# A two-layer gated cross-attention and expert kernel: five program blocks become one, groups of four tiles become groups of two and four

## The chip, the cores and the metric

The kernel runs on one core of one Trainium2 chip. The core has a matrix engine (PE in the profile; its weight loads are PEld), a vector engine (DVE), a scalar engine (ACT), GpSimd (POOL), a queue processor for transfers (SP), and 16 DMA engines. The metric is the device time of one execution in microseconds, taken as the median of several runs.

## The reference, cut to what matters

64 sequences of 64 positions with 128 features (`x`), a context of the same shape, and a mask of 64 x 64 x 64. Four steps, each added to `x`:

```python
x = x + tanh(g_xattn[0]) * L0_xattn(layernorm(x), ctx, ctx, mask)   # 16 heads of 8, masked softmax
x = x + tanh(g_ffn[0])   * L0_ffn(layernorm(x))                     # 8 experts 128->512->128, top 1, exact gelu
x = x + tanh(g_xattn[1]) * L1_xattn(layernorm(x), ctx, ctx)         # 16 heads of 8, no mask
x = x + tanh(g_ffn[1])   * L1_ffn(layernorm(x))                     # 16 experts 128->64->128, top 2, 8 slots each
```

In `L0_ffn` a token goes to the expert with the largest gate logit. In `L1_ffn` each sequence gives every expert 8 slots; a token that comes too late gets the expert's last slot back in the collecting step.

## The kernel before

The 4096 tokens are 32 tiles of 128 rows; a tile holds two sequences. The program is a row of blocks, and at the end of a block all engines meet: `setup` (constants), `attention(0)`, `experts0`, `attention(1)`, `moe1`. Within a block each engine has a fixed, in-order list of instructions; semaphores tie the engines together.

**Attention.** The list of an engine is made by `run`: step `(f, every, skew)` does its part for tile t at iteration t + skew. Tiles are loaded and projected in groups of Q = 4. SP loads `x`, `ctx` and the mask. DVE makes the layer norm's sums (`stat`), POOL the factors (`norm`), ACT applies them (`normed`), PE turns the tile (`turn_x` L524), ACT copies it out of the matrix engine's memory, PE multiplies by wq (L565). The context is loaded with tokens on the partitions, turned on PE (`turn_ctx` L532), copied by ACT, and multiplied by wk (L570) and wv (L580). POOL spreads the keys into a block form (`k_blk` L290). `score` (L593, L599): in layer 0 two products of 128 x 128 with the identity write the mask's bias over all of `S_ps`, then four products of 64 x 64 add the scores, one for each half of the queries and of the heads. In the profile a product of f32 is two MATMUL records and a product of bf16 one, so the four are eight records. DVE takes the maximum (L409) and subtracts it (L417), PE turns the result (L610), ACT takes the exponential (L372), PE multiplies by the values (L621), DVE divides (L424, L428), PE turns and projects (L629, L635), DVE adds to `x_all` (L437). The scores have one buffer: the next `score` waits for the subtraction of this tile.

**Router.** 8 to 20 iterations behind, each group is normed again, turned (L543), multiplied by the router (L549); DVE picks the expert (`choose`), PE counts (L555, L557), DVE makes the destination rows, and POOL scatters the normed rows to an expert-sorted array in HBM (`scatter` L310, an indirect transfer).

**experts0.** DVE makes tables of the 39 row tiles (L705 to L732), SP and ACT write zero rows behind each expert's last one (L762, L808), then a rolled loop over the 39 tiles: SP loads rows, PE turns them, POOL copies the expert's first weight (`f_w_now` L784), PE multiplies (L823), DVE adds the bias, ACT takes gelu, PE multiplies (L832), DVE adds, SP stores to `expert_out`. The expert weights (4 MB and more) are loaded by SP in four transfers early in `attention(0)` (L251).

**attention(1)** first fetches: 32 indirect transfers on POOL (L258) gather each token's row of `expert_out` and add it into `x_all`. **moe1**: at its start DVE finds all tokens' slots and ACT all exponentials (L1010), then for 32 tiles `move` builds a 0/1 matrix (POOL `one`, DVE `dispatch`) and multiplies the tile by it (PE L1053); 16 steps of experts (L1067, L1078) follow each half, and `back` brings the results to the tokens.

## Time and profile before

| what | value |
|---|---|
| median of 3 runs | 669.02 us (665.96 to 738.38) |
| the profiled execution | 671.69 us, its span 669.8 us |
| PE busy | 527.0 us, 79% of the span |
| DVE busy | 382.2 us, 57% |
| POOL busy | 361.2 us, 54% |
| ACT busy | 303.2 us, 45% |
| mean granted clock | 0.89 |

The span is the time from the first to the last instruction. A busy time is an average over stages with different limits, so the page's slices and a table by stage are read before any one line.

### The profile page before, as it was taken

To read this page: it belongs to the slowest core of one execution; us is meant where nothing else is said; L and a number is where in the kernel's file an instruction comes from. 1 tells how busy PE (TensorE), PEld (TensorE's weight loads), DVE (VectorE), ACT (ScalarE), POOL (GpSimd) and SP (SyncE) were. 2 spreads that over 40 slices of the span, in tenths; PEclk is the share of its full clock that TensorE was granted. 3 is DMA by queue.
4 is the path that set the end of the run, shared out by engine and by line. 5 is a ranking of instruction groups with operands and counts; after the bars stand their busy time and mean duration, and the time that the engine had idled before them with its cause. 6 is when DMAs were issued, how large, how long until landed. Compare 5 with 4: busy or idle time off the path is not lost. (4 is left out here: it accounts for less than half of the span.)

```text
span 669.8 us, 16837 instructions
## 1 busy us (share of the span) xinstructions
PE 527.0 (79%) x5478; PEld 359.0 (54%) x5479; DVE 382.2 (57%) x1041; ACT 303.2 (45%) x694; POOL 361.2 (54%) x451
## 2 busy tenths in 40 slices
PE   1489999989999423999980479999999995288888
PEld 0235655666656313988970235665666664164444
DVE  3077778888776414444441147787787874433336
ACT  0435666645534201333330345556666553655554
POOL 2455545657763651222217899999775511164346
PEclk9999999999989555999995579999999995559999
DMA  5921011000000112122217211211000000000012
GB/s 152 306 64 41 18 42 25 25 2 17 10 14 18 37 39 79 54 61 63 59 51 165 40 16 33 33 34 28 7 2 1 2 2 0 0 1 1 20 33 76
DMA packets 48469, 28.04 MB, mean 42 GB/s; under 512 B 11920, under 2 KB 45328, under 8 KB 48400
## 3 DMA queue, kind: packets, MB, share of 16 engines
q1 hardware_dynamic: 42048, 22.14, 11.6%
q0 software_dynamic: 5632, 4.20, 3.5%
q10 hardware_dynamic: 720, 0.80, 0.4%
q8 instruction: 41, 0.67, 0.4%
q14 instruction: 28, 0.23, 0.1%
HBM read 19.39 MB, written 7.73 MB: 40 GB/s over the span
## 5 line engine op out<-in xcount | busy, mean ns | idle before, releaser
L290 POOL TENSOR_TENSOR k_blk<-kT,columns 128x512 f32<-128x512 f32 x128 | 139.3, 1174 | 71.1 <-PE S_ps L599 65.6
L409 DVE TENSOR_REDUCE maxes<-S_ps 128x8 f32<-128x512 f32 x128 | 87.4, 683 | 54.5 <-PE S_ps L599 54.1
L372 ACT ACTIVATE probT<-T_ps 128x512 f32<-128x512 f32 x128 | 76.5, 598 | 73.9 <-PE T_ps L610 72.7
L417 DVE TENSOR_TENSOR prob<-S_ps,maxes 128x512 f32<-128x512 f32 x128 | 88.5, 691 | 4.4
L610 PEld LDWEIGHTS T_ps<-columns,prob 128*128 128x128 f32 x512 | 55.8, 143 | 58.9 <-issue 51.1
L610 PE MATMUL T_ps<-columns,prob 128*128 128x128 f32 x512 | 83.9, 286 | 4.3 <-DVE prob L417 4.3
L599 PE MATMUL S_ps<-k_blk,qT 64*64 64x512 f32 x512 | 72.4, 636 | 6.4 <-POOL k_blk L290 4.8
L621 PE MATMUL A_ps<-v_blk,probT 128*64 128x18 f32 x2048 | 71.3, 212 | 0.2
L621 PEld LDWEIGHTS A_ps<-v_blk,probT 128*64 128x64 f32 x2048 | 64.9, 138 | 11.0 <-issue 11.0
L784 POOL COPY f_w_now<-f_w 128x512 f32 x39 | 23.9, 613 | 72.1 <-PE f_H_ps L823 59.4
L258 POOL DMA_INDIRECT x_all<-expert_out,row_int x32 | 50.6, 1582 | 17.0 <-POOLq L647 10.4
L739 DVE TENSOR_TENSOR f_hid<-f_H_ps,f_b 128x512 f32<-128x512 f32 x39 | 27.0, 691 | 41.0 <-PE f_Y_ps L832 32.8
L801 ACT ACTIVATE f_hid<-f_hid 128x512 f32<-128x512 f32 x39 | 24.6, 630 | 53.5 <-DVE f_hid L739 53.5
L333 ACT ACTIVATE xn<-x_all,shift,rstd 128x128 f32<-128x128 f32 x64 | 30.4, 485 | 37.9 <-POOL shift L278 37.8
L823 PE MATMUL f_H_ps<-f_rowsT,f_w_now 128*128 128x128 f32 x312 | 45.5, 292 | 0.7
L445 DVE BATCH_NORM_STATS2 stats<-x_all 128x6 f32<-128x128 f32 x64 | 18.4, 287 | 46.5 <-DMA x_all<-expert_out,row_int 27.0
L832 PE MATMUL f_Y_ps<-f_w,f_hid 128*128 x312 | 43.0, 281 | 0.6 <-ACT f_hid L801 0.4
L823 PEld LDWEIGHTS f_H_ps<-f_rowsT,f_w_now 128*128 128x128 f32 x312 | 40.4, 202 | 4.5 <-issue 4.1
L832 PEld LDWEIGHTS f_Y_ps<-f_w,f_hid 128*128 128x128 f32 x312 | 38.0, 192 | 3.7 <-issue 3.7
L999 POOL TENSOR_SCALAR m_other<-row_constants,m_slot,m_gap 128x128 f32<-128x128 f32 x32 | 26.1, 820 | 21.6 <-DVE m_combine L980 20.9
L310 POOL DMA_INDIRECT sorted_rows<-r_xn,r_row x32 | 32.0, 1000 | 9.6 <-issue 9.0
L994 POOL TENSOR_SCALAR m_one<-row_constants,m_sent 128x128 f32<-128x128 f32 x32 | 19.7, 627 | 23.6 <-DVE m_dispatch L961 19.4
(163 smaller groups left out, 919.9 us busy)
## 6 DMA issues: line engine op xcount, KB each, us to landing
ctx_in<-in_ctx SPq DMA_DIRECT2D x16, 256.0 KB
f_rows<-sorted_rows SPq DMA_DIRECT2D x39, 64.0 KB, 1.8
expert_out<-f_done SPq DMA_DIRECT2D x39, 64.0 KB, 1.6
x_all<-in_x SPq DMA_DIRECT2D x8, 256.0 KB, 3.1
f_w<-in_W SPq DMA_DIRECT2D x1, 2048.0 KB, 9.4
out<-m_final SPq DMA_DIRECT2D x32, 64.0 KB, 1.5
mask_in<-in_mask SPq DMA_DIRECT2D x8, 128.0 KB, 2.3
columns<-in_columns ACTq DMA_DIRECT2D x1, 529.5 KB, 5.1
```

Of the source, the lines that this page charges most:

```text
L258: pool.indirect_dma_start(x_all[:, t * D:(t + 1) * D], None, r["expert_out"], bass.IndirectOffsetOnAxis(ap=r["row_int"][:, t:t + 1], axis= ...
L290: last = nc.gpsimd.tensor_tensor(k_blk[:, t % 2, b, :, :], kT[:, q % 2, u, b * S:(b + 1) * S].unsqueeze(1).to_broadcast([P, HP, S]), w["he ...
L310: pool.indirect_dma_start(r["sorted"], bass.IndirectOffsetOnAxis(ap=row[:, t % RING:t % RING + 1], axis=0), r_xn[:, t % RING, :], None).th ...
L333: nc.scalar.activation(xn[:, u, :], x_all[:, t * D:(t + 1) * D], ACT.Identity, bias=shift[:, q % 2, u:u + 1], scale=rstd[:, q % 2, u:u + 1 ...
L372: nc.scalar.activation(probT[:, t % 2, 4 * g:4 * g + 4, :], T_ps[g][:, :, :], ACT.Exp, scale=SCALE).then_inc(probT_ready, 1)
L409: nc.vector.tensor_reduce(maxes[:, t % 2, heads], S_ps[g][:, :, :], X, ALU.max).then_inc(max_ready, 1)
L417: nc.vector.tensor_tensor(prob[:, t % 2, heads, :], S_ps[g][:, :, :], maxes[:, t % 2, heads].unsqueeze(2).to_broadcast([P, HP, S]), ALU.su ...
L599: last = nc.tensor.matmul(S_ps[g][b * S:(b + 1) * S, :, :], qT[rows, q % 2, u, b * S:(b + 1) * S], k_blk[rows, t % 2, b, :, :], start=not ...
L610: last = nc.tensor.transpose(T_ps[g][:, j, :], pair, ident[:, :])
L621: last = nc.tensor.matmul(AV[b * S:(b + 1) * S, t % 2 * HP + j, :], probT[:, t % 2, j, b * S:(b + 1) * S], v_blk[:, q % 2, u, b, j, :], st ...
L823: last = nc.tensor.matmul(H_ps[T.par][:, n, :], w1_now[:, T.par, n * P:(n + 1) * P], rowsT[:, T.par, :], start=True, stop=True)
L832: last = nc.tensor.matmul(Y_ps[T.par][:, 0:D], hid[:, T.par, n, :], w2[:, bass.ds(e, 1), n, :].rearrange("p a c -> p (a c)"), start=n == 0 ...
```

## The change

1. **One block.** `attention`, `experts0` and `moe1` no longer hold blocks; they return an object with one function for each engine. `program` opens one block and calls, on each engine, the functions one after the other: attention 0, a piece `ahead` of attention 1, the experts, attention 1, the second experts. There is no meeting of the engines between them. The constants' setup and the loads of the expert weights are steps within attention's list (`hooks`); the weights come in 18 pieces on ACT's queue. The loops over the 39 tiles are unrolled.
2. **Groups of 2 and 4.** `SIZES` has ten groups for 32 tiles; a `when` function in place of the skew says at which iteration a step stands. The router runs fewer iterations behind.
3. **Context turned on the host side's array.** `ctxT` is loaded with features on the partitions; `turn_ctx` and its copy are gone.
4. **Mask.** Each half of the partitions gets the mask rows of both sequences (two transfers for a group, twice the elements on DVE), and four products of 64 x 64 in place of two of 128 x 128 add it.
5. **Expert results.** Each sorted row carries its token's number in a 129th column. `x` after attention 0 is kept in HBM (`x_mid`), and 39 indirect transfers on POOL add the experts' rows to it as they come; attention 1 then loads `x` from there. The copy of the first weight moves from POOL to ACT.
6. **Ahead.** Keys and values of attention 1's first three groups (8 tiles) are made before the experts; slots and exponentials of `moe1` are found group by group within attention 1, and its first 16 `move` steps stand in attention 1's list behind the last tile.

Its core, cut from the diff:

```diff
+SIZES = (2, 2, 4, 4, 4, 4, 4, 4, 2, 2)
...
+        early = [] if masked else groups[:3]
...
+                sp.dma_start(ctxT[:, g.at(CR), 0:g.n, :],
+                             dram["ctxT"][:, dram_rows(g)].rearrange("d (u p) -> d u p", p=P)).then_inc(ctx_loaded[g.at(CR)], 16)
...
+                for h in range(2):
+                    sp.dma_start(mask_in[h * S:(h + 1) * S, g.at(R), 0:g.n, :, :],
+                                 dram["mask"][dram_rows(g), :].rearrange("(u b q) k -> q u b k", b=2, q=S)).then_inc(mask_loaded[g.at(R)], 16)
...
+            project_k, project_v = tensor_steps(pe, x_banks["q"])
+            for g in early:
+                project_k(g)
+                for u in g.units:
+                    project_v(u)
...
-            def turn_ctx(q):
-                pe.wait_ge(ctx_loaded[q % 2], 16 * (q // 2 + 1))
-                for u in range(Q):
-                    last = nc.tensor.transpose(X_ps[:, u, :], ctx_in[:, q % 2, u, :], ident[:, :])
-                last.then_inc(ctx_turned, 1)
...
-                    for g in range(2):
-                        nc.tensor.matmul(S_ps[g][:, :, :], w["ident_bf"][:, :],
-                                         mask_bias[:, q % 2, u, :].unsqueeze(1).to_broadcast([P, HP, S]),
-                                         start=True, stop=False, skip_group_check=True)
+                    pe.wait_ge(mask_made, g.i + 1)
+                    pe.wait_ge(r["casts"], 1)
+                    for b in range(2):
+                        for h in range(2):
+                            rows = slice(h * S, (h + 1) * S)
+                            nc.tensor.matmul(S_ps[h][b * S:(b + 1) * S, :, :], w["ident_bf"][rows, rows],
+                                             mask_bias[rows, g.at(R), u, b, :].unsqueeze(1).to_broadcast([S, HP, S]),
+                                             start=True, stop=False, skip_group_check=True)
...
-            def weights(T):
-                e = pool.value_load(expert_tab[0:1, bass.ds(T.t, 1)], min_val=0, max_val=E0 - 1)
-                wait(pool, hidden, T.t - 1)
-                pool.tensor_copy(w1_now[:, T.par, :], w1[:, bass.ds(e, 1), :].rearrange("p a c -> p (a c)")).then_inc(w1_ready, 1)
...
+    def gpsimd(pool):
+        pool.wait_ge(done["kept"], 16 * NG)
+        for t in range(MAX_TILES):
+            pool.wait_ge(y_out, t + 1)
+            pool.wait_ge(rows_in[t % RINGS], 16 * (t // RINGS + 1))
+            if t >= DEEP:
+                pool.wait_ge(sent[t % DEEP], 16 * (t // DEEP))
+            pool.indirect_dma_start(r["x_mid"], bass.IndirectOffsetOnAxis(ap=rows[:, t % RINGS, D:RW].bitcast(I32), axis=0),
+                                    out[:, t % DEEP, :], None, compute_op=ALU.add).then_inc(sent[t % DEEP], 16)
...
+        def weights(t):
+            e = eng.value_load(tab[1:2, t:t + 1], min_val=0, max_val=E0 - 1)
+            wait(eng, hidden, t - 1)
+            act.copy(w1_now[:, t % 2, :], w1[:, bass.ds(e, 1), :].rearrange("p a c -> p (a c)")).then_inc(w1_ready, 1)
...
+        after = 2 * NT
+
+        def when(t):
+            return after + 1 + t // 2
+
+        hooks[1].update(
+            sync=lambda sp: [],
+            gpsimd=lambda pool: [(moves[0](pool), ahead_tiles, when)],
+            scalar=lambda act: [(ask_f1, once, lambda _: NT + 4), (moves[1](act), ahead_tiles, lambda t: when(t) + 1)],
+            vector=lambda dve: [(moves[2](dve), ahead_tiles, when)],
+            tensor=lambda pe: [(moves[3](pe), ahead_tiles, when)])
+        first, _ = of(0)
+        then, ahead = of(1)
...
+        @block.tensor
+        def _(pe):
+            first.tensor(pe)
+            ahead.tensor(pe)
+            experts.tensor(pe)
+            then.tensor(pe)
+            second.tensor(pe)
```

Where the instructions now stand. PE's list before, from the last group's router on and the first tile of the experts (`X_ps` is the router's memory, `f_T_ps` and `f_H_ps` are of the experts):

```order
L543 MATMUL X_ps<-columns,r_xn 128x128 x4
L549 MATMUL X_ps<-columns,r_xnT 128x8 x4
L555 MATMUL X_ps<-r_chosen,before_bf 128x32
L557 MATMUL X_ps<-r_chosen,ones_bf 128x32
L557 MATMUL X_ps<-r_chosen,ones_bf 128x24
L557 MATMUL X_ps<-r_chosen,ones_bf 128x16
L557 MATMUL X_ps<-r_chosen,ones_bf 128x8
L114 UNCONDITIONAL_BRANCH
L811 UNCONDITIONAL_BRANCH
L816 MATMUL f_T_ps<-columns,f_rows 128x128 x2
L823 MATMUL f_H_ps<-f_rowsT,f_w_now 128x128 x4
```

and now, from the last group's logits on (`Q_ps` takes keys and values, `col_55` is attention 1's weights, `f_pair` the table of row tiles):

```order
L733 MATMUL X_ps<-r_chosen,before_bf 128x16
L735 MATMUL X_ps<-r_chosen,ones_bf 128x16
L735 MATMUL X_ps<-r_chosen,ones_bf 128x8
L672 MATMUL Q_ps<-ctxT,col_55 128x256
L683 MATMUL Q_ps<-col_55,ctxT 64x64 x8
L672 MATMUL Q_ps<-ctxT,col_55 128x256
L683 MATMUL Q_ps<-col_55,ctxT 64x64 x8
L672 MATMUL Q_ps<-ctxT,col_55 128x512
L683 MATMUL Q_ps<-col_55,ctxT 64x64 x16
L988 MATMUL f_T_ps<-col_a,f_pair 2x128
L994 MATMUL f_T_ps<-col_a,f_rows 128x128 x2
L1001 MATMUL f_H_ps<-f_rowsT,f_w_now 128x128 x4
```

Between the router's last count and the first expert tile stand six more steps of keys and values, and behind them the turn of the table.

ACT's list there, now (`kT` and `v_blk` are the copies of keys and values, `pads` the rows behind each expert's last one; four such transfers stand there):

```order
L496 COPY r_xnT<-X_ps 128x256
L432 ACTIVATE kT<-Q_ps,col_55 128x256
L441 COPY v_blk<-Q_ps 64x32x8 x2
L432 ACTIVATE kT<-Q_ps,col_55 128x256
L441 COPY v_blk<-Q_ps 64x32x8 x2
L432 ACTIVATE kT<-Q_ps,col_55 128x512
L441 COPY v_blk<-Q_ps 64x32x8 x4
L966 TENSOR_LOAD f_filled
L966 ISA x2
L967 ISA
L967 DMA sorted_rows<-pads 128x129
```

The transfers of the pads stand behind all those copies; before, they were the first thing on ACT after the block's start.

PE's list at the end of attention 1, now (`m_X_ps` is a `move`, two of them for x4; `m_H_ps` the first expert step; before, all 18 moves stood between the last `L1046` count of the slots and `m_H_ps`):

```order
L715 MATMUL X_ps<-col_a,r_xn 128x128 x4
L1191 MATMUL m_X_ps<-m_dispatch,r_xn 128x128 x4
L725 MATMUL X_ps<-col_b,r_xnT 128x16 x4
L715 MATMUL X_ps<-col_a,r_xn 128x128 x2
L1191 MATMUL m_X_ps<-m_dispatch,r_xn 128x128 x4
L725 MATMUL X_ps<-col_b,r_xnT 128x16 x2
L1191 MATMUL m_X_ps<-m_dispatch,r_xn 128x128 x4
L715 MATMUL X_ps<-col_a,r_xn 128x128 x2
L1191 MATMUL m_X_ps<-m_dispatch,r_xn 128x128 x4
L744 MATMUL X_ps<-both,before_bf 128x128
L745 MATMUL X_ps<-both,ones_bf 128x64
L725 MATMUL X_ps<-col_b,r_xnT 128x16 x2
```

The moves stand between the steps of the last groups' router.

## Rows read from the trace of the kernel before

**Rows 1.** The page's 40 slices: PE busy and the granted clock, in tenths.

```profile
PE   1489999989999423999980479999999995288888
...
PEclk9999999999989555999995579999999995559999
```

**Rows 2.** Windows, one for a stage: start:end length, busy us of engines, clock, DMA share, GB/s.

```profile
0.00:35.10 35.10, 9.47 (x36) 5.21 (x38) 8.24 (x39) 8.42 (x17) 11.43 (x21) 1.00 0.73 218
35.10:206.80 171.70, 162.76 (x1950) 100.63 (x1951) 135.02 (x306) 92.82 (x182) 100.26 (x123) 0.99 0.09 26
206.80:263.10 56.30, 21.48 (x207) 16.77 (x205) 23.98 (x101) 10.22 (x23) 25.64 (x34) 0.60 0.14 44
263.10:350.00 86.90, 85.63 (x662) 78.41 (x661) 38.04 (x77) 31.78 (x78) 22.70 (x37) 0.97 0.19 56
350.00:388.90 38.90, 8.32 (x32) 4.28 (x33) 6.01 (x25) 6.94 (x15) 31.30 (x28) 0.55 0.49 95
388.90:542.10 153.20, 146.61 (x1876) 95.29 (x1876) 113.26 (x275) 88.56 (x177) 118.78 (x131) 0.98 0.10 17
542.10:596.70 54.60, 31.98 (x254) 24.41 (x255) 28.32 (x125) 26.61 (x108) 17.79 (x33) 0.59 0.00 1
596.70:669.80 73.10, 60.75 (x472) 34.00 (x472) 29.34 (x94) 37.89 (x96) 33.26 (x45) 0.95 0.10 30
```

**Rows 3.** Timeline of the start: start us, us, engine, line, operation [idle before, releaser].

```profile
6.63 0.36 DVE L1163 COPY bv_rows<-columns 128x128 f32<-128x128 f32 x2 [5.54 <-DMA columns<-in_columns]
...
17.73 10.80 SPq L242 DMA_DIRECT2D x_all<-in_x  x1
...
33.16 0.29 DVE L445 BATCH_NORM_STATS2 stats<-x_all 128x6 f32<-128x128 f32 x1 [14.76 <-DMA x_all<-in_x]
...
34.54 0.42 DVE L469 TENSOR_TENSOR mask_bias<-mask_zero,mask_value 128x256 bf16<-128x256 f32 x1
```

**Rows 4.** Groups by line, 100 to 188 us: count | busy us, mean ns | idle before.

```profile
L409 DVE TENSOR_REDUCE maxes<-S_ps 128x8 f32<-128x512 f32 x31 | 21.2, 684 | 7.8 <-PE S_ps L599 7.7
...
L599 PE MATMUL S_ps<-k_blk,qT 64*64 64x512 f32 x128 | 17.4, 614 | 0.0
...
L593 PE MATMUL S_ps<-mask_bias,ident_bf 128*128 128x512 bf16 x30 | 8.9, 379 | 1.4 <-DVE prob L417 1.4
...
L469 DVE TENSOR_TENSOR mask_bias<-mask_zero,mask_value 128x256 bf16<-128x256 f32 x4 | 4.8, 1194 | 0.1
...
L532 PE MATMUL X_ps<-columns,ctx_in 128*128 128x128 f32 x12 | 1.9, 283 | 0.8 <-DVE r_chosen L482 0.8
```

**Rows 5.** Timeline from attention 0 to the experts.

```profile
218.96 0.69 DVE L437 TENSOR_TENSOR x_all<-Y_ps,x_all 128x512 f32<-128x512 f32 x1 [2.65 <-issue]
...
221.37 0.25 PE L557 MATMUL X_ps<-r_chosen,ones_bf 128*128 128x32 bf16 x4
...
227.74 0.25 PE L557 MATMUL X_ps<-r_chosen,ones_bf 128*128 128x32 bf16 x4
...
252.62 4.10 ACTq L808 DMA_DIRECT2D sorted_rows<-f_zeros  x4
```

**Rows 6.** Timeline from the experts to attention 1.

```profile
353.30 1.64 POOL L258 DMA_INDIRECT x_all<-expert_out,row_int  x1 [10.41 <-POOLq L647]
...
371.21 1.04 POOL L276 TENSOR_TENSOR rstd<-mv,minus_half 128x4 f32<-128x4 f32 x1
...
374.75 1.12 PE L524 MATMUL X_ps<-columns,xn 128*128 128x128 f32 x4 [17.56 <-ACT xn L333]
...
379.48 2.04 PE L570 MATMUL Q_ps<-ctxT,columns 128*128 128x512 f32 x2 [0.87 <-ACT qT L349]
...
386.12 2.63 POOL L290 TENSOR_TENSOR k_blk<-kT,columns 128x512 f32<-128x512 f32 x2
```

**Rows 7.** Timeline from attention 1 to the second experts' first step.

```profile
584.53 12.14 PE L1053 MATMUL m_X_ps<-m_dispatch,xn_all 64*128 64x128 f32 x72 [10.00 <-DVE m_dispatch L961]
```

**Rows 8.** The page's transfers: KB each, median us from issue to landing.

```profile
x_all<-expert_out,row_int POOLq DMA_INDIRECT x32, 3.3
```

More of the change, by code:

```diff
@@ L844, in moe1 @@
+def moe1(nc, ctx, space, late, r, x_all, r_xn, tg, out, done):
     PARTS = 2
@@ L1262, with _ @@
+        @block.vector
+        def _(dve):
+            first.vector(dve)
+            experts.vector(dve)
+            then.vector(dve)
+            second.vector(dve)
+        @block.tensor
[5 more added lines that the diff above has]
+            second.tensor(pe)
 def kernel(**inputs):
```

2065 lines of the change are left out of this document (1104 added, 961 removed).

## The prediction, made before the kernel was run

> **What bounds the kernel now.** The page's 40 slices come first [rows 1]: PE is near full in four stretches, and idle, at half the clock, in four others. Windows cut there show each stage's limit [rows 2]. In both attentions and both expert stages PE is busy for 162.76 of 171.7, 146.61 of 153.2, 85.63 of 86.9 and 60.75 of 73.1 us, with the clock at the upper level (0.95 to 0.99): the length there is PE's list. The start (35.1 us) and the three borders (56.3, 38.9, 54.6) make 184.9 us with 71 us of PE work in them, at the borders at 0.55 to 0.60, so about half speed (1.2 GHz): chains of waits, on a slow PE. The timelines [rows 3, 5 to 7] show which wait ends last there. The change is worked out stage by stage, against the span of 669.8; the profiled execution took 671.69, so 1.9 lie outside.
>
> **Start, 35.1 to 21.5 (-13.5).** SP's issue of `x_all` at 17.73 took 10.80, held behind the transfers of the weights; its data is used at 33.16, and the first mask product follows at 35.1 [rows 3]. The weights now go on ACT's queue in pieces. If only that issue's time goes, 24.8 is left; if no transfer is waited for, the constants (6.63 [rows 3]), PE's 9.47 of work [rows 2] and the last 2.0 after the data give 18.1. I take the middle.
>
> **Attention 0, 171.7 to 165 (-7).** The group views of some 16 tiles [rows 4] carry the terms.
> - *Mask products.* Two of 128x128 take 2 x 0.30 = 0.59 a tile. A score's eight records, each 0.614 long, take 1.09 in all, so 4.5 lie side by side. If the four mask products do likewise they take one's 0.30: -0.30 x 32 = -9.5. If they stood one behind the other: 1.19, +0.60 x 32 = +19. I take the first, since the score's products have the same 64x64 shape and 512 columns. The Trainium skill ("TensorEngine Tiling (Array Packing)", Key Properties) has separate tiles run in parallel, but a switch between tilings drain the engine. Before, the full-size mask product and the score's quadrants were two tilings in a row, now one; the switch with the turns behind stays, so by that rule nothing is lost here.
> - *Context turns.* L532 is 12 x 0.16 in 1.9, 0.63 a group, 7 groups behind the start: -4.
> - *DVE.* The mask's three passes run on twice the elements. The subtraction L469 takes 0.42 where POOL is idle [rows 3] and 1.194 in mid-stage [rows 4]. A four-tile group's doubled passes thus cost 1.1 (0.26+0.42+0.42, the first two estimated as L469) to 3.6 more. DVE is busy 135 of 171.7 [rows 2], and waits before L409 for only 7.8 in 16 tiles [rows 4]; but its list is in order, and a lump of 4 to 7 us in front of the next maximum (L409) holds the one score buffer, and PE with it. Eight groups' worth at 1.1 to 3.6 is 9 to 29 us of work, of which most fits in DVE's 37 us of slack: I book +3, up to +13.
> - The router's steps come fewer iterations behind, so 2.5 of PE's work moves in from the border (+2.5), and the first tiles run cold (+1).
> Sum -7; bounds -14 and +28.
>
> **Border 1, 56.3 to 48 (-8.5).** Before: the last mask product at 206.8, last add at 218.96 (+12.2), then counts of three router groups 6.4 apart (221.37, 227.74, two more) [rows 5], tables, zero rows at 252.62, block ends. Now, from the last mask: +11.3 to the last add; three groups' routers remain, of 4, 2 and 2 tiles: 6.4 for the first, 4 each for the small ones: +25.5. Only then, in PE's list, come the keys and values of three groups. A four-tile group takes from 379.48 to 386.1, 7, and small ones some 3.7 [rows 6]: +40. On ACT's list the four pads' transfers, 4.10 [rows 5], stand behind its copies: +44. Their landing, the loads, the table's turn: +48. So the work ahead is in the way here, and only what it saves at border 2 pays for it. If tables and pads run beside it, 36; if each step waits as before, 58.
>
> **Experts, 86.9 (0, give or take 3).** PE is busy 98.5% of it [rows 2], 2.23 a tile. The weight copy takes ACT from 31.78/39 = 0.8 to some 1.5 a tile, the scatter-add POOL to 1.6 (L258's issue [rows 6]): both under 2.23.
>
> **Border 2, 38.9 to 17 (-22).** Gone are the wait to the block's start and the fetches: the first gather is issued at 353.30, and the first group's factors come at 371.21. Gone too are keys, values and `k_blk`, 379.48 to 388.9 [rows 6]: 9.4. What stands there now: last product to last scatter-add landed, 0.3 + 3.3 (the gather's landing [rows 8], plus up to its issue of 1.64), the load of `x` 2.3 (an estimate under the gather's 3.3), statistics of two tiles 0.8 (L445's 0.29 and as little again [rows 3]), factors and normed rows 3 (371.21 to 374.75 for four tiles is 3.5), turn, copy, product, copy for two tiles 2.4 (half of 374.75 to 379.48) [rows 6]; 12.1 and the issue's 1.64 are 13.7, with handshakes and a second small group 17. Bounds 13 and 25. The indirect transfer's 3.3 is the row; the Trainium skill ("DMA: Bandwidth & Descriptors", Anatomy of one DMA, SWDGE path) fits 2.0 us plus bytes by 436e3, so 2.15 for 64 KB: a border 1.1 shorter.
>
> **Attention 1, 153.2 (0).** Context turns -4.3, keys and values of three groups partly off the list -2; router earlier +2.5, the slots' counts +2.5, some DVE waits +1. DVE's 113.26 + 0.6 x 32 = 132 for slots stays below PE's 146.6 [rows 2]. Bounds -6 and +5.
>
> **Border 3, 54.6 to 34 (-20).** Before, exponentials and slots of all tiles stand serially between the last router and the moves, whose 72 records take 12.14 cold [rows 7]. Now only the last groups' are left, and 16 moves are interleaved. What remains: the last add at +11.3 and, one behind the other, routers and moves, 23. Bounds 26 and 40. **Second experts, 73.1**, the same.
>
> Sum: -13.5 -7 -8.5 -22 -20 = -71. Span 598.8, execution 600.7. The median before lies 2.7 under its profiled execution, so **598 us**; own range 585 to 611.
>
> **Rivals.**
> - *A, the forecast* (0.57): 598.
> - *B, attention 0 gives nothing* (0.13): the mask products run in series (+28 to the term taken) and the doubled mask passes at the contended price (+10): 636. For it: L469 at 1.194 against 0.42, so DVE's price depends on what POOL does beside it. Against: the score's 4.5 side by side. By the Trainium skill ("GPSIMD Engine Reference", Specifications) POOL shares memory interfaces with VectorE, contending where an instruction has two inputs there; that speaks against doubling such passes, and the two prices of L469 agree.
> - *C, the borders overlap better* (0.22): pads and tables go beside keys and values (border 1 -12), the moves fill the router's waits (border 3 -7), transfers come early (start -4): 575.
> - *D, the chains stay long* (0.06): with three engines in order and no meeting, each border waits for the slowest list, 10 more at each of four: 638, and with B 676, within 2%.
> - *E, slower* (0.02): the scatter-adds set the pace of the experts. Each waits for earlier ones into the same array; four may be in flight, so 4 x 2.23 = 8.9 of landing is hidden. To eat 71 over 39 tiles, one every 2.23 + 1.82 = 4.05, landing must be 16.2, to be 2% slower 17.6; then 684 and more. The nearest row, 3.3 [rows 8], is far off.
>
> Within 2% means 655.6 to 682.4, 13.4 either side, about what a measurement of this kernel can tell from no change. Faster: A, B, C and D where B doesn't come with it (0.02), 0.94; same: D with B, 0.04; slower 0.02. The range takes in A whole and C at 575 with 5 under it, and of B the half under 632; what is left out is under 2 in 10: 570 to 632.
>
> **What would show it.** Start: the first mask product (L765) at 21.5, and no long issue on SP before it. Attention 0: four L765 products in 0.3, not 1.2; spacing of masks 5.2 a tile; a wait before L765 once a group for DVE's mask pass would be B. Border 1: the last count (L735), then keys and values on PE, and the first L1001 some 22 after; if PE idles behind them for pads, the lists' order matters. Experts: L1001's spacing 2.2; more is E. Border 2: from the last L1010 to the first score (L771) 17. Border 3: moves (L1191) between router steps, first L1207 some 34 after the last score. The prediction fails if attention 0 doesn't shrink, or the borders, together 120 now against 185, lie outside 100 to 140.

## The result, and the profile after

The changed kernel takes 666.39 us (median of 20 runs, 662.59 to 670.55), the kernel before 670.91 (20 runs): the ratio is 0.9933, with a 95% interval of 0.9905 to 0.9962. 598 was forecast, in 570 to 632. So the change gives 0.7% where 11% was forecast.

The profiled execution's span is 665.0 us. The slices of TensorE (PE) and its clock on the page, to be held against [rows 1]:

```profile
PE   2687899798889554999982899989886976868887
...
PEclk9987998999989555999995699987988896559999
```

The borders (5 and 6 in the clock) are shorter, but now 7s and 8s stand inside the two attentions, where nearly only 9s stood before. The windows by stage, cut where those of [rows 2] were cut (first mask product, last mask product, first expert product, last one, first score, last score, first step of the second experts); columns as there:

```profile
0.00:23.80 23.80, 10.18 (x38) 5.18 (x42) 15.16 (x44) 7.77 (x17) 12.15 (x28) 1.00 0.57 157
23.80:206.90 183.10, 158.58 (x2012) 101.52 (x2013) 147.36 (x341) 91.12 (x184) 107.80 (x136) 0.94 0.23 64
206.90:258.80 51.90, 27.38 (x264) 19.07 (x263) 18.46 (x87) 15.16 (x36) 23.97 (x32) 0.61 0.19 57
258.80:348.00 89.20, 83.09 (x661) 76.72 (x661) 38.05 (x77) 57.87 (x115) 57.49 (x37) 0.98 0.41 55
348.00:365.90 17.90, 3.46 (x8) 1.75 (x8) 4.44 (x25) 4.00 (x10) 10.25 (x21) 0.61 0.57 143
365.90:544.40 178.50, 155.39 (x1825) 99.74 (x1824) 121.30 (x335) 90.93 (x214) 91.31 (x130) 0.90 0.07 18
544.40:588.00 43.60, 30.67 (x247) 24.01 (x246) 26.10 (x135) 19.57 (x78) 18.09 (x42) 0.60 0.00 1
588.00:665.00 77.00, 63.54 (x474) 35.50 (x472) 29.29 (x94) 38.17 (x97) 33.43 (x45) 0.90 0.10 28
```

| stage | before | forecast | after | with the repairs of the last experiment |
|---|---|---|---|---|
| start | 35.1 | 21.5 | 23.8 | 23.4 |
| attention 0 | 171.7 | 165 | **183.1** | 164.7 |
| border 1 | 56.3 | 48 | 51.9 | 51.6 |
| experts | 86.9 | 86.9 | 89.2 | 91.2 |
| border 2 | 38.9 | 17 | 17.9 | 18.3 |
| attention 1 | 153.2 | 153 | **178.5** | 158.2 |
| border 3 | 54.6 | 34 | 43.6 | 42.5 |
| second experts | 73.1 | 73.1 | 77.0 | 74.1 |
| span | 669.8 | 598.8 | 665.0 | 624.0 |

Start and borders gave 47.7 us of the 64 forecast for them. The two attentions took 36.7 us back, where they were to give 7. PE's busy time fell in attention 0 (158.6 against 162.8) and grew in attention 1 (155.4 against 146.6, at a lower clock), but in both PE now stands idle, for 24.5 and 23.1 us where it was 8.9 and 6.6.

**Attention 0.** The list of waits of PE there has one line that matters (in all us, times, longest); before, the same wait (the turn of the probabilities for VectorE's `prob`) was 1.5 us in two pieces:

```profile
PE T_ps L782 <- DVE prob L537: 14.7, 9, 4.2
```

The timeline of one such place, a four-tile group in mid-stage (one of the two groups of six in which the small pass `mask_value` was over 2 us):

```profile
124.30 0.41 PE L765 MATMUL S_ps<-mask_bias,ident_bf 64*64 64x512 bf16 x4 [0.58 <-issue]
...
125.05 0.69 DVE L585 TENSOR_REDUCE mask_all<-mask_zero 128x8 f32<-128x512 f32 x1
...
125.77 2.23 DVE L586 TENSOR_SCALAR mask_value<-mask_all 128x8 f32<-128x8 f32 x1
125.91 2.05 POOL L363 TENSOR_TENSOR k_blk<-kT,col_a 128x512 f32<-128x512 f32 x2
...
128.03 0.69 DVE L588 TENSOR_TENSOR mask_bias<-mask_zero,mask_value 128x512 bf16<-128x512 f32 x1
...
130.11 1.12 PE L782 MATMUL T_ps<-col_a,prob 128*128 128x128 f32 x4 [0.93 <-DVE prob L537]
...
132.86 0.64 PE L765 MATMUL S_ps<-mask_bias,ident_bf 64*64 64x512 bf16 x4
```

`mask_value` handles eight numbers a partition and takes 2.23 us. It ends when GpSimd's `k_blk`, which it overlaps, ends (127.96). The maximum and the subtraction stand behind it, so PE's next turn is late, and from there PE's products take longer: the same four mask products last 0.41 at 124.30 and 0.64 at 132.86, the turns 0.66 elsewhere and 1.12 here. This tile took 8.6 us from mask to mask where 5.2 was forecast. The longest wait, 4.2 us before the turn at 59.26, is another one: 3.2 us of it stay until the filling of the pads is moved, in the last experiment.

**Attention 1.** PE's waits there; before, behind the first score, they were 6.6 us in all, in pieces of up to 1.0:

```profile
PE X_ps L708 <- DVE ranks_of L643: 4.5, 2, 2.2
PE X_ps L744 <- DVE both L634: 4.4, 4, 1.4
PE T_ps L782 <- DVE prob L537: 3.2, 2, 1.7
PE X_ps L715 <- DVE ranks_of L643: 2.2, 1, 2.2
```

And one of the places in the timeline:

```profile
479.06 0.23 PE L744 MATMUL X_ps<-both,before_bf 128*128 128x128 bf16 x1 [1.43 <-DVE both L634]
...
483.78 0.28 DVE L643 TENSOR_TENSOR ranks_of<-X_ps,both 128x128 f32<-128x128 f32 x1
...
484.21 0.63 PE L708 MATMUL X_ps<-col_a,xn 128*128 128x128 f32 x4 [2.24 <-DVE ranks_of L643]
...
485.60 1.09 PE L715 MATMUL X_ps<-col_a,r_xn 128*128 128x128 f32 x4 [0.77 <-ACT xnT L466]
...
487.34 1.56 PE L751 MATMUL Q_ps<-xnT,col 128*128 128x512 f32 x2
...
488.83 1.09 PE L771 MATMUL S_ps<-k_blk,qT 64*64 64x512 f32 x8
```

The slots' ranks (L744) are written to `X_ps` at the start of the iteration in which, for groups of four, the next group's `x` is turned into the same memory (L708). VectorE reads the ranks only behind two more maxima and subtractions and the division, so the turn waits 2.24 us, the router's turn another 0.77, and the score comes 9.6 us after the last one. The slots' counts are new in this stage's list, and the iteration that they were given is the one of that turn.

### The profile page after: what moved, and what is told of

The parts are those of the page before. It is cut to its first block, busy times and chain, and to the rows that moved or that the text cites. A ratio compares the mean times of both kernels' runs of the same rounds, so it can differ in the third digit from the quotient of the medians.

```text
span 665.0 us, 16440 instructions
## 1 busy us (share of the span) xinstructions
PE 532.3 (80%) x5514; PEld 363.5 (55%) x5514; DVE 400.1 (60%) x1138; ACT 324.6 (49%) x748; POOL 354.5 (53%) x469
## 4 chain that ended last, share of the span: by engine, by line
PE 60%; DVE 16%; issue 11%; ACT 5%; DMA 4%; POOL 2%; ACTq 1%; SPq 1%; DVEq 0%; POOLq 0%
PE S_ps L771 8%; PE T_ps L782 7%; PE A_ps L795 6%; PE f_H_ps L1001 6%; DVE maxes L529 5%; PE f_Y_ps L1010 4%; PE Q_ps L751 3%; PE Q_ps L683 3%; PE m_H_ps L1207 3%; PE X_ps L725 3%; PE Q_ps L672 2%; PE Y_ps L810 2%; PE m_X_ps L1191 2%; DVE prob L537 2%; PE m_X_ps L1244 2%
## 5 line engine op out<-in xcount | busy, mean ns | idle before, releaser
L363 POOL TENSOR_TENSOR k_blk<-kT,col_a 128x512 f32<-128x512 f32 x128 | 131.8, 1050 | 144.0 <-PE S_ps L771 143.9
L782 PE MATMUL T_ps<-col_a,prob 128*128 128x128 f32 x512 | 89.1, 300 | 19.2 <-DVE prob L537 19.2
L782 PEld LDWEIGHTS T_ps<-col_a,prob 128*128 128x128 f32 x512 | 59.5, 150 | 80.7 <-issue 55.7
L960 POOL DMA_INDIRECT x_mid<-f_out,f_rows x39 | 60.7, 1555 | 45.4 <-DVE f_out L929 44.2
L795 PEld LDWEIGHTS A_ps<-v_blk,probT 128*64 128x64 f32 x2048 | 67.0, 141 | 11.6 <-issue 11.3
L409 POOL DMA_INDIRECT sorted_rows<-r_xn,row x32 | 32.1, 1005 | 18.2 <-issue 8.7
L460 ACT ACTIVATE xn<-x_all,shift_by,rstd 128x128 f32<-128x128 f32 x64 | 30.7, 484 | 21.3 <-POOL shift_by L384 21.3
L1147 POOL TENSOR_SCALAR m_other<-row_constants,r_slot,r_gap 128x128 f32<-128x128 f32 x32 | 26.2, 825 | 21.9 <-DVE m_combine L1127 21.2
L441 ACT COPY v_blk<-Q_ps 64x256 f32<-64x256 f32 x64 | 23.8, 372 | 27.0 <-PE Q_ps L683 26.5
L982 ACT ACTIVATE f_hid<-f_hid 128x512 f32<-128x512 f32 x39 | 24.6, 630 | 20.0 <-DVE f_hid L920 19.9
L1140 POOL TENSOR_SCALAR m_one<-row_constants,r_sent 128x128 f32<-128x128 f32 x32 | 19.2, 611 | 22.2 <-DVE m_dispatch L1101 22.1
L490 ACT ACTIVATE r_xn<-x_all,r_shift,r_rstd 128x128 f32<-128x128 f32 x64 | 27.8, 485 | 2.9 <-POOL r_shift L401 2.9
```

What stands on the lines that cost most here:

```text
L363: last = nc.gpsimd.tensor_tensor(k_blk[:, t % 2, b, :, :], kT[:, g.at(R), t - g.first, b * S:(b + 1) * S].unsqueeze(1).to_broadcast([P, HP ...
L409: pool.indirect_dma_start(r["sorted"], bass.IndirectOffsetOnAxis(ap=row[:, t:t + 1], axis=0), r_xn[:, t, :], None).then_inc(scattered[t % ...
L460: nc.scalar.activation(xn[:, g.at(XR), u, :], x_of(t), ACT.Identity, bias=shift_by[:, g.i % 2, u:u + 1], scale=rstd[:, g.i % 2, u:u + 1]). ...
L782: last = nc.tensor.transpose(T_ps[h][:, j, :], pair, ident[:, :])
L795: last = nc.tensor.matmul(AV[b * S:(b + 1) * S, m + j, :], probT[:, t % 2, j, b * S:(b + 1) * S], v_blk[:, g.at(R), t - g.first, b, j, :], ...
L960: pool.indirect_dma_start(r["x_mid"], bass.IndirectOffsetOnAxis(ap=rows[:, t % RINGS, D:RW].bitcast(I32), axis=0), out[:, t % DEEP, :], No ...
```

## The experiments

Ratios are to the kernel before, on the same chip; the changed kernel's is 0.9933. The kernel before took 667.5 to 672.9 us on these chips, so ratios are to be compared and not medians. Stage lengths are those of one profiled execution of each run, cut as above. With unchanged lists attention 1 was 176.2 to 185.0 us in them and attention 0 182.1 to 184.3 (168.6 to 171.6 with GpSimd's wait), so a difference of 3 us in one stage says little by itself.

### Slots at the head of VectorE's iteration

```diff
-            steps = [(maximum(0), tiles, shift(0)), ...
+            steps = [] if masked else [(slots, groups, turned_at(12)), (assign, groups, turned_at(11))]
+            steps += [(maximum(0), tiles, shift(0)), ...
```

> The changed kernel, but in attention 1 VectorE's slot steps (assign, slots) stand at the head of their iteration, before the two maxima, instead of behind them. Theory X: attention 1 grew from 153.2 to 178.5 us because the slots' ranks and the next group's turn of x share one bank (X_ps) and VectorE reads the ranks late: once a group TensorE waits 1.4 us for both and 2.2 us for ranks_of, and its clock then falls. So attention 1 goes to 155 to 162 us, the total down by 15 to 22 us, and the waits of L708, L744 and L715 on VectorE vanish. Rival G (the groups of two and the shorter router lag as such cost it): attention 1 stays within 4 us of 178.5 and the total within 4 us.

657.66 us, ratio 0.9844 (0.9767 to 0.992). The waits on `ranks_of` and `both` are gone, yet attention 1 is 174.6 us: PE now waits 9.8 us for `prob` and 5.0 more at the score. The forecast of 155 to 162 was missed, and by length alone the rival G (within 4 us of 178.5) fits as well; the groups of four below rule it out. The steps now stand in front of what PE needs. The profile's span is 10.2 us shorter, 3.9 of it in attention 1 and 4.1 in border 3.

### No mask passes

```diff
-                step(nc.vector.tensor_scalar(mask_zero[:, 0:n, :, :], mask_in[:, at, 0:n, :, :], 0.0, None, ALU.is_equal))
...
+                dve.sem_inc(mask_made, 1)
```

> The changed kernel without VectorE's four mask passes (the mask's bias is filled with zeros once, so no masking is computed; the transfers and the mask products stay). Theory M: attention 0 grew from 171.7 to 183.1 us instead of shrinking because the mask passes, one lump of some 3.6 us for a group of four on VectorE, hold the subtraction for which TensorE waits (14.7 us), with the clock falling behind each wait. So attention 0 goes to 163 to 168 us, the total down by 14 to 20 us. Rival R (the router's steps next to the turn of x): attention 0 falls by less than 6 us.

649.39 us, 0.9694 (0.9637 to 0.9751). Attention 0 is 166.6 us, as Theory M had it, and the clock there 0.98. So VectorE's mask passes, 26.3 us of work, cost attention 0 16.5 us, more than the 11.4 that it grew by.

### The mask as before, within the changed kernel

```diff
-                            nc.tensor.matmul(S_ps[h][b * S:(b + 1) * S, :, :], w["ident_bf"][rows, rows], ...
+                        nc.tensor.matmul(S_ps[h][:, :, :], w["ident_bf"][:, :],
```

> The changed kernel with the mask as before: one row set, two 128x128 products a tile. TensorE's mask products take 0.59 us a tile instead of 0.41 or less (+6 to +9 us of work in all), VectorE's passes about 1.2 us less for a group of four (-9 us in all). Theory M (VectorE's lump is what TensorE waits for): attention 0 falls by 2 to 8 us. The prediction's view (TensorE's list bounds): it grows by 6 to 9 us.

661.3 us, 0.9869 (0.9808 to 0.9929). (With the products go one of the two transfers and half of the passes' elements, as before.) Attention 0 is 171.7 us, 11.4 less than with the new mask: the prediction's view has the wrong sign here, and the effect is larger than Theory M's 2 to 8. (Attention 1, with the same lists as in the changed kernel, was 185.0 us in this profile, at a clock of 0.88; its waits were longer by the same kind.)

### The new mask alone, within the kernel before

```diff
-                    for g in range(2):
-                        nc.tensor.matmul(S_ps[g][:, :, :], w["ident_bf"][:, :],
...
+                    for b in range(2):
+                        for g in range(2):
+                            rows = slice(g * S, (g + 1) * S)
+                            nc.tensor.matmul(S_ps[g][b * S:(b + 1) * S, :, :], w["ident_bf"][rows, rows],
...
```

> The kernel before with the new mask alone: both sequences' rows on both halves, four 64x64 products a tile. The prediction's view: attention 0 falls by 5 to 9 us from 171.7. Theory M: it stays within 3 us or grows, since what TensorE saves it waits for VectorE's doubled passes.

669.84 us, 1.0028 (0.9982 to 1.0075): no change in all. But attention 0 is 164.6 us against 171.7, just the 7 us that the prediction's view wanted; the start was 2.4 us and border 3 3.6 us longer in this profile. The same edit gives 7 us in one kernel and costs 11 in the other. The grouped view of VectorE's mask passes tells them apart. Of the kernel before with the new mask:

```profile
L471 DVE TENSOR_TENSOR mask_bias<-mask_zero,mask_value 128x512 bf16<-128x512 f32 x7 | 7.9, 1133 | 0.2
...
L469 DVE TENSOR_SCALAR mask_value<-mask_all 128x8 f32<-128x8 f32 x7 | 1.9, 271 | 0.2
```

and of the changed kernel:

```profile
L588 DVE TENSOR_TENSOR mask_bias<-mask_zero,mask_value 128x512 bf16<-128x512 f32 x6 | 7.3, 1212 | 0.2
L586 DVE TENSOR_SCALAR mask_value<-mask_all 128x8 f32<-128x8 f32 x6 | 7.0, 1162 | 0.2
```

The same operation on the same eight elements takes 0.27 there and 1.16 here (0.17 to 2.33 in the six). But `mask_bias` is nearly as long there as here, and so the passes' sum differs by only 6 us (20.1 and 26.3) where the stages differ by 18.5. Longer passes alone do not make the difference: what counts is what stands behind them and what PE waits for then.

### Slots one and two iterations later

```diff
-                steps += [(slots, groups, turned_at(12)), ... (assign, groups, turned_at(11))]
+                steps += [(slots, groups, turned_at(13)), ... (assign, groups, turned_at(12))]
-                steps += [(rank_slots, groups, turned_at(11))]
+                steps += [(rank_slots, groups, turned_at(13))]
```

> The changed kernel, in attention 1 with assign one iteration later and the slots' products two iterations later (slots one later), so that their ranks no longer hold X_ps when the next group's x is turned, and VectorE's order within an iteration stays. Theory X: the 11 us of TensorE's waits on both and ranks_of vanish and VectorE delays nothing else, so attention 1 goes from 178.5 to 158 to 166 us, total down by 12 to 20 us from the changed kernel. Rival (moving the waits only moves them, as it did with the slots at the head of the iteration, where attention 1 stayed at 174.6): 172 us or more.

668.17 us, 0.9878 (0.9809 to 0.9946). Attention 1 is 168.1 us: between the two. The total fell by far less than these 10.4 us; in the profile border 1 was 6.1 us longer (an idle time of ScalarE, see "Moves eight iterations later") and border 3 2.6. The waits on `ranks_of` and `both` are gone and PE waits 10.2 us for `prob` in their place. The timeline shows the same thing as in attention 0, on operations that take 0.17 us elsewhere:

```profile
456.29 2.05 POOL L363 TENSOR_TENSOR k_blk<-kT,col_a 128x512 f32<-128x512 f32 x2 [2.54 <-PE S_ps L771]
456.55 0.81 DVE L645 SCALAR_TENSOR_TENSOR r_slot<-rank_at,base 128x4 f32<-128x4 f32 x1
...
457.39 0.97 DVE L646 TENSOR_SCALAR over<-rank_at 128x4 f32<-128x4 f32 x1
...
458.30 1.26 POOL L389 TENSOR_TENSOR x_all<-x_all,row_constants 128x512 f32<-128x512 f32 x1
458.40 1.18 DVE L647 TENSOR_TENSOR r_sent<-over,r_slot 128x4 f32<-128x4 f32 x1
...
460.96 0.66 PE L782 MATMUL T_ps<-col_a,prob 128*128 128x128 f32 x4 [2.85 <-DVE prob L537]
```

Each of VectorE's three small operations ends as one of GpSimd's ends (the two products of `k_blk` at 457.3 and 458.3, the addition at 459.6), and PE waits 2.85 us.

### Late slots and the old mask together

Both edits as above.

> The changed kernel with the slots late and the mask as before. If the two losses are separate (VectorE's mask lump in attention 0, X_ps in attention 1) the gains add up: attention 0 at 170 to 174 us, attention 1 at 158 to 166, total 638 to 650 us. If one slow stage only hands its delay to the next, under 8 us below the changed kernel with the old mask alone (661.3).

655.98 us, 0.9704 (0.964 to 0.9768); attention 0 174.5, attention 1 170.7. Both stages gain, 8.6 and 7.8 us, each some 3 less than alone (11.4 and 10.4), and attention 1 misses its 158 to 166, the total its 638 to 650. By the medians it is 5.3 us under the old mask alone, which fits the rival's "under 8"; by the ratios (0.9869 and 0.9704) it is 11.

### Useless products in PE's waits

```diff
-                         (turn_av, units, unit_end(2)), (logit, groups, turned_at(8)), (turn_r, groups, turned_at(7)),
+                         (turn_av, units, unit_end(2)), (logit, groups, turned_at(8)), (turn_r, groups, turned_at(7)), fill(FILLS[1], turned_at(7), 1),
...
```

> The changed kernel with useless products of TensorE (128x128 with 224 columns, results overwritten) in its list where it waits in the attentions: 6 behind the turn of x, 6 behind the router's turn, in attention 1 also 12 before the turn of x and 10 before the slots' products, some 0.1 us each at full clock. Theory C (the waits are short, but behind each the granted clock falls to the lower level, and at it the list takes twice as long; by the mean clocks 0.94 and 0.90 that is up to 11 and 18 us): the clock in both attentions rises to 0.97 or more, and the total falls by 5 to 15 us although work is added. Rival (the waits themselves are the loss, the clock is a by-product): the total stays or rises by up to 10 us.

672.72 us, 0.9996 (0.996 to 1.0032). The profiled execution took 679.82, with the same idle time of ScalarE in border 1. Attention 1, whose line in the windows reads

```profile
377.70:557.50 179.80, 165.81 (x2059) 114.94 (x2058) 122.40 (x335) 91.68 (x214) 91.47 (x130) 0.97 0.07 18
```

has its clock back (0.97 against 0.90) and is as long as without the filling (178.5). PE gained the speed where it was halved, and spent it on the filling (234 products more of some 0.1 us). In attention 0 the clock stayed at 0.94 and the stage grew from 183.1 to 187.6. So the forecast of Theory C failed, and the rival's held. But what the lower clock costs by itself is not shown: the filling was as large as the gain.

### Groups of four

```diff
-SIZES = (2, 2, 4, 4, 4, 4, 4, 4, 2, 2)
+SIZES = (4,) * 8
```

> The changed kernel with eight groups of four (as before) in place of ten of two and four. Theories M and X hold the group size innocent: attentions within 5 us of 183.1 and 178.5; start and borders longer by 3 to 10 us in all, total up by 0 to 8 us. Rival G (the small groups disturb the order at the start and the end of each attention): attentions 8 us or more shorter in sum and the total down by over 4 us.

675.45 us, 1.0023 (0.9978 to 1.0067). Attentions 180.6 and 178.3, start 26.5, border 1 62.1 (three groups ahead are 12 tiles there, and ScalarE's idle time, 6.4 us, is in it). The small groups are not what the attentions lost by. By the ratios they are worth about 6 us in all; how much of that is the idle time is not shown.

### GpSimd's `k_blk` left out

```diff
+                if t < 2:
...
+                else:
+                    pool.sem_inc(kblk_ready, 1)
```

> The changed kernel without the building of the keys' block form on GpSimd (k_blk is made for the first two tiles only, so the scores are not the reference's; all waits and products stay). Theory P: VectorE's mask and slot steps are long because GpSimd's k_blk runs beside them (mask_value, 128x8, took 1.16 us in the changed kernel and 0.26 in the kernel before with the new mask). Then mask_value falls to 0.2, mask_bias to 0.7 us, attention 0 goes from 183 to 164 to 172 us, attention 1 from 178 to 165 to 175 (its waits on X_ps stay), total down by 15 to 30 us. Rival (VectorE's doubled element count is the cost, not its neighbour): mask_value above 0.6 us, total down by under 8 us.

648.15 us, 0.9671 (0.9598 to 0.9743). `mask_value` falls to 0.172 us, `mask_bias` to 0.693, the passes' sum from 26.3 to 14.3 us, attention 0 to 164.9. Attention 1 stays (181.8), against the 165 to 175 of Theory P, with 12 us of waits on `ranks_of` and `both`: there `X_ps` comes first.

### One wait more on GpSimd

```diff
                 wait(pool, scored, t - 1)
+                wait(pool, max_ready, 2 * (t - 2) + 1)
```

> The changed kernel with one wait more: GpSimd builds the k_blk of tile t only once VectorE has taken the first maximum of tile t-2, so that the 2.05 us of k_blk lie beside VectorE's reads of S_ps (maxima and subtractions, 0.68 us each, which a busy GpSimd has not lengthened) and not beside its mask and slot steps. Theory P: attention 0 183 to 168 to 175, attention 1 178 to 165 to 175, total down by 8 to 22 us. Rival (k_blk comes too late for the score and becomes the wait itself): waits of L771 or L765 on k_blk, total no lower.

647.25 us, 0.9653 (0.9587 to 0.9719). Attention 0 is 168.8; attention 1 is 177.1 and misses its 165 to 175. The mask passes, grouped:

```profile
L585 DVE TENSOR_SCALAR mask_zero<-mask_in 128x512 f32<-128x512 int32 x6 | 5.5, 916 | 0.0
L589 DVE TENSOR_TENSOR mask_bias<-mask_zero,mask_value 128x512 bf16<-128x512 f32 x6 | 4.2, 694 | 0.2
...
L587 DVE TENSOR_SCALAR mask_value<-mask_all 128x8 f32<-128x8 f32 x6 | 1.5, 251 | 0.2
```

`k_blk` now lies beside VectorE's maxima and subtractions of `S_ps`, which keep their 0.68 and 0.69 us. The passes' sum is 18.0 us against 26.3. The contention is not gone: `mask_zero` takes 0.92 where it took 0.61, and the router's `r_level` 0.78 where it took 0.19. But it is away from most of what PE waits for. A wait that was added took 19 us off. PE waits 4.0 us for `k_blk` in eight small pieces; that is the price.

### The wait and the late slots

The last edit and that of the late slots.

> The changed kernel (new mask) with GpSimd's wait and the late slots. If P and X are separate causes: attention 0 at 168 to 175, attention 1 at 156 to 163 us, total 630 to 645. If they are the same delay seen twice: no lower than the better of the two alone.

632.4 us, 0.9437 (0.9373 to 0.9501). Attention 0 168.6, attention 1 157.5 at a clock of 0.98. Alone the late slots gave attention 1 10.4 us and the wait 1.4, which is nothing that one profile can tell; together 21.0: each alone leaves the other's wait standing.

### The same with the old mask

As before, and the mask's edit above.

> As the run with GpSimd's wait and the late slots, but with the mask as before. If the contention was why the new mask cost 11 us in the changed kernel while it gave 7 in the kernel before, then with the contention gone the new mask is ahead by 2 to 8 us of this one; if the old mask stays ahead, the doubled passes themselves are too long for this order. Total 635 to 650 us.

639.55 us, 0.9557 (0.9485 to 0.9628), attention 0 174.3. With GpSimd's wait the new mask is 5.7 us ahead in attention 0, much as in the kernel before (7.1).

### Moves eight iterations later

```diff
-            return after + 1 + t // 2
+            return after + 9 + t // 2
```

> The changed kernel with GpSimd's wait and the late slots (632 us), and the 16 moves started eight iterations later, behind most of the last groups' router instead of between its steps. The prediction put border 3 (last score to the second experts' first step) at 34 us, it measured 43.6 to 45.9. Theory V (the moves stand in the way: the last add comes 19 us after the last score where 11.3 was forecast, because matrices and products of moves stand before it in three lists): the last add comes by +14, border 3 falls by 2 to 7 us. Rival (the moves fill waits of the router's chain): border 3 grows by 3 to 8 us.

644.4 us, 0.9558 (0.947 to 0.9646). Border 3 is 50.3 us against 45.9: the rival holds, the moves fill waits. (Border 1 was 6 us longer in this profile with the same instructions: ScalarE stood idle once for 7.20 us, released by an event that the trace calls remote. It is in five of the profiles, 5.8 to 7.2 us long: this one, the late slots with either mask, the useless products and the groups of four. Its cause is open. For that reason the total is no measure of the moves.)

### No keys and values ahead

```diff
-        early = [] if masked else groups[:3]
+        early = []
```

> The 632 us kernel without the piece ahead: keys and values of attention 1's first three groups are made within attention 1, as before. The prediction's terms: the piece costs 14.6 us at border 1, of which some 10 to 13 on the way to the first expert, and saves 9.4 at border 2 and 2 in attention 1. So border 1 50.7 to 38 to 42, border 2 18.3 to 25 to 29, attention 1 +2 to +6: total -4 to +6 us. Rival (the router's and tables' chain covers the piece): border 1 stays above 46, total up by 8 or more.

634.63 us, 0.9439 (0.9352 to 0.9527): no difference to 0.9437. Border 1 is 43.3 against 51.9, border 2 23.4 against 18.3, attention 1 158.8 against 157.5, each a little outside its forecast. The prediction's reading of the piece ahead was right in kind (what it saves behind the experts, it costs before them) and too large in size: 8.6 us at border 1, not 14.

### The new mask and the wait, and the wait alone, in the kernel before

The line of GpSimd's wait above, with and without the new mask.

> The kernel before with the new mask and GpSimd's wait for the first maximum. Theory P holds for it too if its mask and router steps meet k_blk: its mask_bias took 1.08 us there and r_level 0.47 where 0.69 and 0.19 are free of it; attention 0 164.6 to 158 to 163, total 1 to 3% under the kernel before. Rival (its order leaves enough room, so the contention is off the path): within 0.7% of the new mask alone.

665.56 us, 0.9927 (0.9886 to 0.9968). Attention 0 is 164.4, as without the wait (164.6), so the forecast of 158 to 163 failed: `mask_bias` stayed at 1.08. The total is 1.0% under the new mask alone, which its rival (0.7%) doesn't have either; in the profiles border 3 is shorter (53.5 against 58.1), and why is open.

> The kernel before, unchanged but for GpSimd's wait for the first maximum. Theory P: VectorE's mask_bias 0.81 to 0.43 us, r_chosen 0.41 to 0.19; but TensorE's waits on VectorE in attention 0 are under 5 us, so the total falls by 0 to 6 us. Rival: k_blk comes later and the total rises by over 3 us (POOL also gathers the experts' rows there, 1.6 us each, in attention 1).

670.92 us, 0.996 (0.9921 to 0.9999). Attention 0 168.1 against 171.7. The router's operations fell (`r_chosen` 0.414 to 0.192), the mask's did not (`mask_bias` 0.809 and 0.811). Three of its eight take some 1.45 instead of 0.42, and each lies beside another work of GpSimd, the addition of a bias to `x_all`:

```profile
105.88 1.27 POOL L283 TENSOR_TENSOR x_all<-x_all,row_constants 128x512 f32<-128x512 f32 x1
105.98 1.45 DVE L470 TENSOR_TENSOR mask_bias<-mask_zero,mask_value 128x256 bf16<-128x256 f32 x1
```

So the contention was in the kernel before as well, mostly off the path.

### The pads' filling later, and then the mask in halves

```diff
-            vec.memset(r0["pads"][:, :, :], 0.0).then_inc(r0["ids_ready"], 1)
...
+        def pad_late(_):
+            vec.memset(r0["pads"][:, :, :], 0.0).then_inc(r0["ids_ready"], 1)
...
+            vector=lambda dve: [..., (pad, once, lambda _: 4), (pad_late, once, lambda _: 35)],
```

> The 632 us kernel (GpSimd's wait, late slots, new mask) with the filling of the pads (VectorE, 1.7 us and two waits) moved from the fifth iteration of attention 0, right behind a mask lump, to its end. There the subtraction waits 3.2 us once and the tile takes 10 us instead of 5.5. Lump theory: attention 0 falls by 3 to 5 us, total 627 to 630. Rival: the wait goes to the mask lump and the total stays within 1 us.

(SP's transfer of the pads moves with it, from iteration 6 to 40.) 627.41 us, 0.9393 (0.9342 to 0.9443); attention 0 165.5 against 168.6, the wait of 3.2 us gone. These are the lump theory's numbers; the ratio (0.9437 before) has not moved clear of its interval.

```diff
-                steps += [(rows, groups, turned_at(10)), (mask, groups, head(-4))]
+                steps += [(rows, groups, turned_at(10)), (mask, units, lambda u: u.group.first - 4 + u.k)]
```

> As the run before, and the mask's four passes made for two tiles at a time in two successive iterations instead of for four at once: the same elements, lumps half as long, four more fixed costs of 0.2 us for a group. Lump theory: TensorE's waits on prob in attention 0 (5.9 us) fall under 2 and attention 0 by another 2 to 6 us. Rival (the sum of VectorE's work counts, not its pieces): attention 0 grows by 0 to 3 us.

626.9 us, 0.9383 (0.9328 to 0.9437), no difference to the run before; attention 0 164.7, where PE's waits on `prob` fell from 3.5 to 2.5 us. The forecast (under 2 us, the stage another 2 to 6 shorter) was missed. This kernel is the fastest, 6% under the kernel before. Its two attentions in the windows:

```profile
23.40:188.10 164.70, 150.93 (x2008) 98.69 (x2007) 141.19 (x363) 90.76 (x184) 105.85 (x136) 0.99 0.24 69
...
349.20:507.40 158.20, 143.59 (x1827) 93.66 (x1827) 119.84 (x330) 89.98 (x214) 91.51 (x130) 0.97 0.08 20
```

## Why the prediction was wrong, step by step

- **Start** (21.5, measured 23.8): inside its bounds of 18.1 and 24.8, near the one at which only SP's long issue goes; the middle was a choice. **Border 2** (17, measured 17.9): right, built from the chain of steps that is left.
- **Border 1** (48, measured 51.9): the mechanism was right. From the last mask product the last add came at +12.0 (forecast +11.3), the last count at +26.7 (+25.5), the end of keys and values at +41 (+40). The 4 us are missing behind ScalarE's transfers of the pads: PE stood idle for 8.96 us until the first rows had landed.
- **Attention 0** (165, measured 183.1): the step that failed is "a lump of 4 to 7 us in front of the next maximum ... I book +3, up to +13". With the old mask the changed kernel has 171.7, where the forecast's other terms (-4, +2.5, +1) give 171.2; so the whole miss is in the mask. Its products did overlap, 0.41 us for four and not 0.30: -6 and not -9.5. Its passes on VectorE, booked at +3, then cost some +17 (11.4 and 6). Their own work was put well: 26.3 us against 16.8, the low end of the 9 to 29 more. Two things were not in it. It was set against VectorE's idle time of the whole stage (37 us), while PE waits for the one subtraction behind the lump. And what an operation takes depends on what GpSimd does at that moment (`mask_value`: 0.27 or 1.16 us for the same eight elements), which the prediction knew as two prices and did not place in the order. With GpSimd's wait the stage takes 168.8, with `k_blk` left out 164.9. That the last kernel's 164.7 is the forecast's 165 is in part luck: it has two repairs more, and the products gave less than booked. (The stage's upper terms, +19, -4, +13, +2.5 and +1, add up to +31 and not to its stated bound of +28; the measured +11.4 lies within either.)
- **Attention 1** (153, measured 178.5): the step that failed is "some DVE waits +1", with its reason that VectorE's 132 us of work stay below PE's 146.6. It compares sums of work. The slots' counts were priced as work of PE (2.5 us), without the memory that they go to and who reads it when. The order of the changed kernel has it: the slots' ranks and the turn of `x` fall into one iteration. That cost 10.4 us (late slots), and the contention of `k_blk` with VectorE's slot steps, which shows only when the first is gone, another 10.6: with both repairs the stage takes 157.5. The 25 us lie far outside the stage's bounds of -6 and +5.
- **Border 3** (34, measured 43.6): the largest term that stays wrong. It took the last add at +11.3; it came at +19.0, and from it to the second experts' first step another 24.6 us passed, where 23 were booked:

```profile
558.23 0.64 PE L804 MATMUL Y_ps<-col_a,av 128*128 128x128 f32 x2
...
559.20 1.86 PE L725 MATMUL X_ps<-col_b,r_xnT 128*128 128x16 f32 x8 [0.34 <-ACT r_xnT L496]
...
561.10 0.21 ACT L500 COPY r_logits<-X_ps 128x64 f32<-128x64 f32 x1 [2.04 <-PE X_ps L725]
561.21 0.38 ACT L483 COPY avT<-Y_ps 128x256 f32<-128x256 f32 x1
...
563.41 0.42 DVE L556 TENSOR_TENSOR x_all<-Y_ps,x_all 128x256 f32<-128x256 f32 x1 [4.75 <-PE Y_ps L810]
...
588.04 1.12 PE L1207 MATMUL m_H_ps<-m_slotsT,f_gate 128*64 128x256 f32 x4
```

  What was missed is in front of the add. The moves were suspected of it, but with them eight iterations later the add came at +17.0 against +17.9 and the border grew: they fill waits. The rows show one part: the last tiles' turned values are ready at 558.87, but their copy (`avT`) stands in ScalarE's list behind the copy of the router's logits, which waits 2.04 us for PE's product. So 2.3 us of the 7.7 pass there. No run moves that copy, and the rest is open.
- **Experts** (86.9, measured 89.2) and **second experts** (73.1, measured 77.0): the first within its bound of 3; the second, forecast as unchanged, are 3.9 longer, at a mean clock of 0.90 against 0.95.
- **The clock.** Mean 0.94 and 0.90 in the attentions say that 12% and 20% of their time ran at 1.2 GHz, where 0.99 and 0.98 said 2% and 4%. If PE's list bounded all of it, that would be up to 11 and 18 us (an estimate). The clock followed the waits: where both went, it went back to 0.97 and more. How much of the loss is the waits' own and how much the clock's behind them, no run separates.

Rival B named attention 0, with half of its mechanism (VectorE's contended price) right and the other half (mask products in series) wrong; it had 0.13 and 636 us. It booked 10 us for what cost 14 in attention 0 alone (183.1 against 168.8 with GpSimd's wait), and nothing in attention 1. By the Trainium skill ("GPSIMD Engine Reference", Specifications) GpSimd shares its interfaces to the on-chip memory SBUF with VectorE, in contention with VectorE's instructions that have two inputs there or run in a two-port mode. The trace agrees and adds which of this kernel's are touched: `TENSOR_TENSOR` (`mask_bias` 0.69 to 1.49 us), `SCALAR_TENSOR_TENSOR` (`r_slot` 0.16 to 0.81) and `TENSOR_SCALAR` (`mask_value` 0.17 to 2.33) with all inputs in SBUF, while the `TENSOR_REDUCE` of the mask (0.69) and what reads `S_ps` (0.68 and 0.69) are as long beside GpSimd's work as without it. In which mode an instruction ran, no trace shows.

## What to carry to other kernels

In a stage like attention 0, where one engine is 95% busy, waits of 1 to 4 us once a group were more than the whole gain. So cost a change of it by the order at the instruction that the busy engine waits for next, not by sums of work. Ask of each step that moves which buffer it writes, who frees that buffer, and what stands before the freeing operation; and ask what GpSimd does beside every short VectorE operation, since one wait that moves it elsewhere was worth 19 us here. An edit that gives 7 us in one order can cost 11 in another: measure it alone in both.

## What the runs showed of the hardware that was not expected

- VectorE's `mask_value` on 128x8 elements took 0.17 us free and up to 2.33 us beside GpSimd's `k_blk` (2.05 us). It did not slow down in proportion: in the rows above it ended when an instruction of GpSimd did (128.00 and 127.96).
- Behind a wait of PE of 2.24 us, before the turn at 484.21, the next turns took 1.09 and 1.06 us instead of 0.66; it was 0.66 again at 489.85. Not every wait does this: behind 1.04 us, at 154.90, the turn took 0.66. With filled waits the mean clock of attention 1 went from 0.90 to 0.97; that of attention 0 stayed at 0.94.
- Four 64x64 products of bf16 with 512 columns took 0.41 us from the first's start to the last's end, against 0.59 for two of 128x128.
